# A 1-core kernel of two interleaved passes: all four written orders merged anew, other sample orders, 51 slots kept instead of 42

## The reference

```python
def _gn(v, G=32, eps=1e-5):                       # 32 groups of 24 channels, each over a whole image
    g = v.reshape(B_, H_, W_, G, C_ // G)
    m = jnp.mean(g, axis=(1, 2, 4), keepdims=True)
    s = jnp.var(g, axis=(1, 2, 4), keepdims=True)
    return ((g - m) / jnp.sqrt(s + eps)).reshape(v.shape)

xc = conv2d(xc, conv1_w, conv1_b)                 # 1x1, 768 -> 16 channels
pooled = jnp.mean(xc, axis=(2, 3))
h = pooled @ H_w.T + H_b                          # 4 experts, the two largest kept
g = jax.nn.softmax(jnp.where(mask, h, -jnp.inf), axis=1)
for i in range(E):                                # resize by 2**i, one 3x3 conv, resize back
    ...
gw = jnp.reshape(g, (E, g.shape[0], 1, 1, 1))
out = jnp.sum(Es * gw, axis=0)
out = conv2d(out, conv2_w, conv2_b)               # 1x1, 16 -> 768 channels
x = x + _L0_conv_ref(_gn(x), ...)
```

## Time and profile before

| | |
|---|---|
| median of 3 runs | 1445.71 us (1445.31 to 1447.31) |
| profiled execution, its own time | 1443.26 us |
| its span in the profile | 1441.5 us |
| instructions | 23374 |

### The profile page before, as it was taken

How to read it: one execution, slowest core, us unless ns; L and a number is a source line. 1 busy time by engine, 2 the same in 40 slices (tenths; PEclk the granted TensorE clock), 3 DMA queues, 4 the chain that set the end, 5 groups by cost and what they waited for, 6 DMA issues and landing times.

```text
span 1441.5 us, 23374 instructions
## 1 busy us (share of the span) xinstructions
PE 1108.7 (77%) x8380; PEld 722.4 (50%) x8380; DVE 1028.1 (71%) x2747; ACT 661.8 (46%) x1549; POOL 301.5 (21%) x390
## 2 busy tenths in 40 slices
...
GB/s 342 260 349 316 298 371 315 179 392 345 398 383 414 391 379 352 378 404 404 402 414 409 393 387 284 383 416 416 415 366 390 395 415 415 416 416 416 366 416 386
DMA packets 188159, 539.96 MB, mean 375 GB/s; under 512 B 12810, under 2 KB 12810, under 8 KB 188044
## 3 DMA queue, kind: packets, MB, share of 16 engines
...
...
## 4 chain that ended last, share of the span: by engine, by line
PE 34%; DMA 31%; DVE 18%; ACT 6%; issue 5%; SPq 4%; POOL 1%; ACTq 0%; DVEq 0%; POOLq 0%
DMA x_sb<-in_x 16%; DMA out<-x_sb 15%; PE ring_ps L690 15%; DVE stats L958 9%; PE img_ps L707 8%; DVE x_sb L1042 7%; PE ring_ps L812 5%; SPq L524 3%; ACT xT L834 3%; PE conv_ps L767 2%; SPq L497 1%; PE conv_ps L773 1%; PE ring_ps L799 1%; ACT unread_squares L862 1%; PE ring_ps L721 1%
## 5 line engine op out<-in xcount | busy, mean ns | idle before, releaser
L1042 DVE TENSOR_TENSOR x_sb<-x_sb,ring_ps 128x768 f32<-128x768 f32 x512 | 461.9, 950 | 297.2 <-PE ring_ps L812 169.4
L958 DVE BATCH_NORM_STATS2 stats<-x_sb 128x6 f32<-128x192 f32 x1792 | 473.1, 344 | 43.7 <-DMA x_sb<-in_x 24.7
L812 PE MATMUL ring_ps<-w,es 128*128 128x512 f32 (+1 forms) x1024 | 358.4, 470 | 170.0 <-DVE x_sb L1042 145.3
L834 ACT COPY xT<-ring_ps 128x1024 f32<-128x1024 f32 x384 | 377.2, 1012 | 194.1 <-PE ring_ps L690 132.7
L690 PE MATMUL ring_ps<-ident,x_sb 128*128 128x128 f32 x3072 | 403.5, 285 | 31.6 <-ACT xT L834 11.5
L690 PEld LDWEIGHTS ring_ps<-ident,x_sb 128*128 128x128 f32 x3072 | 352.8, 146 | 108.2 <-issue 59.2
L812 PEld LDWEIGHTS ring_ps<-w,es 128*128 128x128 f32 x1024 | 199.8, 241 | 324.6 <-DVE x_sb L1042 227.6
L707 PE MATMUL img_ps<-xT,w 128*32 128x256 f32 x3072 | 218.3, 393 | 16.6 <-ACT xT L834 14.5
L862 ACT ACTIVATE unread_squares<-x_sb 128x192 bf16<-128x192 f32 x256 | 93.7, 366 | 172.8 <-DVE x_sb L1042 101.7
L898 ACT CAST es<-ring_ps 64x1024 fp32r<-64x1024 f32 x64 | 63.3, 1005 | 201.1 <-PE ring_ps L800 169.6
L624 POOL TENSOR_SCALAR taps<-experts,gates 128x400 f32<-128x400 f32 x16 | 20.5, 1283 | 602.1 <-DVE bias_es L1027 599.9
...
## 6 DMA issues: line engine op xcount, KB each, us to landing
x_sb<-in_x SPq DMA_DIRECT2D x128, 1536.0 KB, 11.3
out<-x_sb ACTq DMA_DIRECT2D x256, 768.0 KB, 10.2
x_sb<-in_x SPq DMA_DIRECT2D x172, 768.0 KB, 9.8
...
wl_raw<-in_L_conv_convl_w SPq DMA_DIRECT2D x8, 9.0 KB
gate_w<-in_L_conv_H_w SPq DMA_DIRECT2D x8, 0.2 KB
...
b_raw<-in_L_conv_conv_b SPq DMA_DIRECT2D x2, 3.0 KB
```

The lines of the kernel that those rows point to most:

```text
L812: last = nc.tensor.matmul(flat_ps[:, buf, part], es4[:, pair_of, QN * n + q], w2[:, part], start=True, stop=True)
L834: nc.scalar.copy(xT[:, at % XT], ring_ps[:, TURN["T", a, n] % RING]).then_inc(xT_copied, 1)
L958: ins = nc.vector.bn_stats(stats[:, c, g, :], group)
L1042: nc.vector.tensor_tensor(x_sb[:, n, 2 * half + q % 2, :], x_sb[:, n, 2 * half + q % 2, :], flat_ps[:, TURN["E", b, t] % RING, 0:D], ALU.a ...
```

## The change

Nothing but text tables changes: the two sample orders, `KEPT`, `TRANSFERS`, `PE_ORDER`, `ACT_ORDER` and `DVE_ORDER`. No instruction of the computation is added or removed, apart from the loads that kept slots save. `KEPT` goes from 42 slots to 51, so that the R transfers go from 172 halves to 154.

```diff
-A_ORDER = [12, 0, 4, 8, 3, 2, 1, 13, 9, 5, 7, 14, 6, 10, 11, 15]
-B_ORDER = [3, 2, 1, 0, 4, 7, 5, 6, 10, 9, 11, 8, 14, 13, 15, 12]
+A_ORDER = [12, 0, 4, 8, 3, 2, 1, 9, 13, 5, 7, 10, 6, 14, 11, 15]
+B_ORDER = [3, 2, 0, 1, 5, 7, 4, 6, 9, 11, 8, 10, 15, 14, 12, 13]
...
-KEPT = {1: 8, 2: 3, 3: 2, 6: 1, 7: 8, 10: 7, 11: 5, 15: 8}
+KEPT = {1: 7, 2: 7, 3: 4, 5: 4, 6: 3, 7: 8, 11: 8, 14: 2, 15: 8}
```

The loads (the old text of the same stretch, then the new):

```diff
-L2.7:1 L1.0:5 L1.1:2 L1.2:3 L1.3:1 L1.4:7 R3.2.0:4.0 R3.2.1:4.1 R3.3.0:0.0 R3.3.1:0.1 L1.5:6 R3.4.0:4.0 R3.4.1:4.1
-L1.6:12 L1.7:10 R3.5.0:0.0 R3.5.1:0.1 R3.6.0:4.0 R3.6.1:4.1 R3.7.0:0.0 R3.7.1:0.1 R2.3.0:0.0 R2.3.1:4.0 R2.4.0:4.1
-R2.4.1:0.1 R2.5.0:9.0 R2.5.1:9.1 R2.6.0:11.0 R2.6.1:8.0 R2.7.0:8.1 L13.0:4 L13.1:0 R2.7.1:11.1 L13.2:9 L13.3:8
-L13.4:11 L13.5:5 L13.6:2 L13.7:3 R0.0.0:1.0 L9.0:7 L9.1:6 L9.2:12 L9.3:10 L9.4:1 L9.5:2 L9.6:3 L9.7:5 L5.0:11 L5.1:8
-L5.2:9 L5.3:0 L5.4:4 L5.5:3 L5.6:5 L5.7:1 L7.0:2 L7.1:10 L7.2:12 L7.3:6 L7.4:7 L7.5:1 L7.6:5 R0.0.1:3.0 R0.1.0:3.1
-R0.1.1:4.0 R0.2.0:4.1 L7.7:0 R0.2.1:3.0 L14.0:9 L14.1:8 R0.3.0:3.1 R0.3.1:4.0 R0.4.0:4.1 R0.4.1:11.0 R0.5.0:11.1
...
+L2.7:1 R3.4.0:5.0 R3.4.1:5.1 R3.5.0:1.0 R3.5.1:1.1 R3.6.0:4.0 R3.6.1:4.1 R3.7.0:0.0 R3.7.1:0.1 L1.0:3 L1.1:2 L1.2:5
+L1.3:1 L1.4:4 L1.5:0 L1.6:9 L1.7:8 R2.7.0:11.0 R2.7.1:11.1 R0.0.0:10.0 R0.0.1:10.1 R0.1.0:12.0 R0.1.1:12.1 R0.2.0:6.0
+R0.2.1:6.1 R0.3.0:7.0 R0.3.1:7.1 R0.4.0:11.0 R0.4.1:11.1 R0.5.0:10.0 R0.5.1:10.1 L9.0:8 R0.6.0:12.0 R0.6.1:12.1 L9.1:6
+R0.7.0:7.0 L9.2:11 R0.7.1:7.1 R1.7.0:10.0 R1.7.1:10.1 L9.3:12 L9.4:7 L9.5:3 L9.6:2 L9.7:5 L13.0:1 L13.1:4 L13.2:0
+L13.3:9 L13.4:2 L13.5:5 L13.6:10 L13.7:3 L5.0:7 L5.1:11 L5.2:12 L5.3:6 L5.4:8 L5.5:3 L5.6:10 L5.7:2 L7.0:5 L7.1:0
+L7.2:9 L7.3:1 L7.4:4 L7.5:2 L7.6:10 L7.7:3 R5.4.0:8.0 R5.4.1:8.1 R5.5.0:7.0 R5.5.1:7.1 R5.6.0:11.0 R5.6.1:11.1
+R5.7.0:12.0 R5.7.1:12.1 L10.0:6 L10.1:8 L10.2:7 L10.3:11 L10.4:12 L10.5:5 L10.6:0 L10.7:9 L6.0:1 L6.1:4 L6.2:2 L6.3:10
+L6.4:3 L6.5:0 L6.6:9 L6.7:5 L14.0:12 L14.1:7 R4.0.0:11.0 R4.0.1:11.1 L14.2:6 L14.3:8 R4.1.0:11.0 R4.1.1:11.1 L14.4:5
+L14.5:9 R4.2.0:11.0 L14.6:0 R4.2.1:3.0 R4.3.0:3.1 R4.3.1:11.1 L14.7:10 R4.4.0:11.0 R4.4.1:3.0 R4.5.0:3.1 R4.5.1:11.1
...
+R6.3.0:1.0 R6.3.1:1.1 R6.4.0:4.0 R6.4.1:4.1 R6.5.0:2.0 R6.5.1:2.1 R6.6.0:1.0 R6.6.1:1.1 R6.7.0:4.0 R6.7.1:4.1
+R9.0.0:2.0 R9.0.1:2.1 R9.1.0:1.0 R9.1.1:1.1 R9.2.0:4.0 R9.2.1:4.1 R9.3.0:2.0 R9.3.1:2.1 R9.4.0:1.0 R9.4.1:1.1
...
```

TensorE's order at the setup, around samples 7, 5, 4 and 6, and around samples 11 and 9 (new text; of the old one only the setup):

```diff
-V Z12 T12.0-5 M12.0-3 T12.6-9 M12.4-7 T12.10 M12.8-9 T12.11-13 M12.10-11 T12.14-15 M12.12-14 T12.16-18 M12.15 T12.19
-M12.16-18 T12.20 M12.19 T12.21-23 M12.20-21 Z0 T0.0 M12.22-23 T0.1-5 M0.0-2 T0.6-7 W M0.3-4 T0.8 M0.5 T0.9 M0.6-9
...
+V T12.0-2 Z12 T12.3-5 M12.0-2 T12.6 M12.3-4 T12.7 M12.5-6 T12.8 M12.7 T12.9-10 M12.8 T12.11 M12.9-10 T12.12 M12.11
+T12.13-14 M12.12 T12.15 M12.13-14 T12.16 M12.15 T12.17-18 M12.16 T12.19 M12.17-18 T12.20 W M12.19 T12.21 M12.20 T12.22
...
+M5.21 T5.23 T7.0 M5.22 T7.1 M5.23 T7.2 G1 Z7 T7.3 H1 M7.0-3 T7.4-6 M7.4 T7.7 M7.5-6 T7.8 M7.7 T7.9 M7.8 T7.10 M7.9
+T7.11 C5.0-6 M7.10-11 T7.12-13 X5.0-1 M7.12-13 E5.0-11 X5.2 E5.12-15 X5.3 E5.16-23 T7.14 E5.24-25 M7.14 T7.15 E5.26-27
...
+X6.2 T14.22-23 M14.22-23 G2 H2 T11.0 E6.12-15 X6.3 E6.16-23 T11.1-2 C9.0-6 E6.24-31 X9.0-1 E9.0-1 Z11 E9.2-3 T11.3
+M11.0-1 E9.4-7 M11.2-3 T11.4 E9.8-9 T11.5 M11.4 T11.6 E9.10-11 M11.5 X9.2 M11.6 T11.7-8 E9.12-13 M11.7 T11.9 M11.8
...
```

VectorE's order at the setup and around the first gates:

```diff
-B12.0.0-27 B12.1.0-27 V B12.2.0-27 B12.3.0-27 F12 B0.0.0-27 B0.1.0-27 B0.2.0-27 B0.3.0-27 F0 B4.0.0-27 W B4.1.0-27
-B4.2.0-27 B4.3.0-27 F4 B8.0.0-27 B8.1.0-27 B8.2.0-27 B8.3.0-27 F8 B3.0.0-27 B3.1.0-27 B3.2.0-27 B3.3.0-27 F3 P0 G0
...
+B12.0.0-13 V B12.0.14-27 B12.1.0-27 B12.2.0-27 B12.3.0-27 F12 B0.0.0-27 B0.1.0-27 B0.2.0-27 B0.3.0-13 W B0.3.14-27 F0
+B4.0.0-27 B4.1.0-27 B4.2.0-27 B4.3.0-27 F4 B8.0.0-27 B8.1.0-27 B8.2.0-27 B8.3.0-27 F8 B3.0.0-27 B3.1.0-27 B3.2.0-27
+B3.3.0-27 F3 P0 B2.0.0-6 G0 B2.0.7-27 B2.1.0-27 B2.2.0-27 B2.3.0-27 F2 L3 A3.0-30 B1.0.0-13 L2 A3.31 B1.0.14-27 A2.0-15
...
```

More of the change, by code:

```diff
@@ L65 @@
[L65 to L74, removed]
@@ L131 @@
-C12.6 E15.20-31 X12.0-1 E12.0-13 X12.2 E12.14-15 X12.3 E12.16-31
+V T12.0-2 Z12 T12.3-5 M12.0-2 T12.6 M12.3-4 T12.7 M12.5-6 T12.8 M12.7 T12.9-10 M12.8 T12.11 M12.9-10 T12.12 M12.11
+T12.13-14 M12.12 T12.15 M12.13-14 T12.16 M12.15 T12.17-18 M12.16 T12.19 M12.17-18 T12.20 W M12.19 T12.21 M12.20 T12.22
+M12.21 T12.23 M12.22 T0.0 M12.23 T0.1-2 Z0 T0.3-5 M0.0-5 T0.6-8 M0.6 T0.9 M0.7-8 T0.10 M0.9 T0.11-12 M0.10 T0.13
+M0.11-12 T0.14 M0.13 T0.15 M0.14 T0.16 M0.15 T0.17-18 M0.16 T0.19-20 M0.17 T0.21 M0.18-19 T0.22 M0.20-21 T0.23 Z4
@@ new lines @@
+T10.12 M10.11 T10.13-14 M10.12 T10.15 M10.13-14 T10.16 M10.15 T10.17-18 M10.16 T10.19 M10.17-18 T10.20 M10.19 T10.21-22
+M10.20 T10.23 M10.21-22 E4.0-2 M10.23 Z6 E4.3 T6.0-3 M6.0-2 T6.4 M6.3 T6.5 E4.4-5 M6.4 T6.6 M6.5 E4.6-7 M6.6 T6.7-8
+M6.7 T6.9-10 M6.8 T6.11 M6.9-10 T6.12 M6.11 T6.13 M6.12 T6.14 E4.8-9 M6.13 T6.15 M6.14 T6.16-17 M6.15 T6.18 E4.10-11
+M6.16-17 X4.2 M6.18 E4.12-13 T6.19 E4.14-15 X4.3 M6.19 T6.20-22 M6.20 T6.23 M6.21-22 T14.0 M6.23 T14.1 E4.16-17 C6.0
+T14.2 E4.18-19 C6.1-2 E4.20-21 C6.3-6 E4.22-23 Z14 T14.3-5 M14.0-2 E4.24-28 M14.3-4 E4.29 M14.5 E4.30-31 T14.6-8 M14.6
@@ new lines @@
+T14.9 M14.7-8 T14.10 M14.9 T14.11 M14.10 X6.0-1 M14.11 T14.12-13 E6.0 T14.14 M14.12-13 E6.1-2 T14.15 M14.14 E6.3 T14.16
+E6.4 M14.15 T14.17 M14.16 E6.5-6 T14.18 M14.17 E6.7 T14.19 M14.18 E6.8 T14.20 M14.19 E6.9-10 T14.21 M14.20 E6.11 M14.21
+X6.2 T14.22-23 M14.22-23 G2 H2 T11.0 E6.12-15 X6.3 E6.16-23 T11.1-2 C9.0-6 E6.24-31 X9.0-1 E9.0-1 Z11 E9.2-3 T11.3
+M11.0-1 E9.4-7 M11.2-3 T11.4 E9.8-9 T11.5 M11.4 T11.6 E9.10-11 M11.5 X9.2 M11.6 T11.7-8 E9.12-13 M11.7 T11.9 M11.8
+T11.10 E9.14-15 M11.9 X9.3 M11.10 T11.11 E9.16-17 T11.12 M11.11 T11.13 E9.18-19 M11.12 T11.14 M11.13 T11.15 E9.20-21
@@ L132 @@
+E12.12-15 X12.3 E12.16-31 X13.0-1 E13.0-11 X13.2 E13.12-15 X13.3 E13.16-31
 """
 ACT_ORDER = """
[L138 to L141 removed]
@@ L177 @@
[L177 to L179 removed]
+S12.0.28-31 S12.1.28-31 S12.2.28-31 S12.3.28-30 T12.0 S12.3.31 T12.1-2 S0.0.28-29 D12 S0.0.30-31 S0.1.28-30 T12.3-6
+S0.1.31 T12.7 S0.2.28 T12.8-10 S0.2.29 T12.11 S0.2.30 T12.12 S0.2.31 T12.13-15 S0.3.28 T12.16-18 S0.3.29 T12.19 S0.3.30
```

202 lines of the change are left out of this document (96 added, 106 removed).

## The result

The changed kernel takes 1459.32 us (median of 4 runs, 1458.62 to 1459.74), the kernel before 1445.51 beside it. The ratio is 1.0099 with a 95% interval of 1.0078 to 1.0121: slower by 1%, where 1432.6 was forecast, and 1.3 us above the range. The profiled execution has a span of 1458.0 against 1441.5, 16.5 us more.

The account below looks back on a forecast made before the run. Transfers, by bytes and by time below their 416 GB/s rate, were taken as the bound: 650 to sample 5's first store + 748.5 + 30 = 1428.4 us span, 1432.6 as measured median; own range 1420 to 1442, full range 1404 to 1458.

Parts of the forecast that it names:

- Traffic: Whole kernel: 51 slots kept instead of 42, 9 fewer reloads, 14.2 MB, 34.0 us less at 416 GB/s.
- Opening: Start to first store: VectorE's new order saves 6 us, bounds 0 and 9.7, first store at 271.4 us.
- W's move: Opening: W falls into VectorE's wait before the fold of sample 0, saving 4 of its 6.7 us.
- Before the first store: Up to the first store: 50 slots moved instead of 53, 11.3 us of transfers lost.
- To T9.0: First store to sample 9's first transpose: 57 slots, 215.5 us, plus 11 lost, bounds 0 and 19; T9.0 at 498.
- The run of pass A: T9.0 to sample 5's first store: 152 us, bounds 142 and 160, 28 slots moved, 46 us without transfers.
- the 8 us to the end of F9: Run of pass A, its first term: F9 ends some 8 us after T9.0.
- the 35.5 for a sample: Run of pass A: three samples at 35.5 us each, 106.5 us together.
- The rest: After sample 5's first store: 198 slots, 748.5 us, transfer-bound, plus 30 us of losses, bounds 10 and 50.
- Slower, 1459: Rival: samples 6 and 9 go through three places with hops of 32 us, adding 26 us; chance 0.22.
- Better overlap: Rival, 1405 us: no loss before T9.0, run of pass A 142, sample 4's hops hidden; chance 0.20.
- The saved bytes come back: Rival, 1445 us: first stretch behind the first store at 382 GB/s, +8, and hops 5 more; chance 0.11.

Follow-up runs that it names:

- Runs 3 and 4: Changed kernel with four kept slots fewer, read again: of sample 5 in the transfer gap, 1457.47 us; of sample 15 where transfers are full, 1476.71 us.
- Run 1: Changed kernel with only ScalarE's opening order edited, sample 0's statistics that need L0.5 put behind later steps of sample 12: 1450.86 us, ratio 1.0037.
- run 2: Changed kernel with W back in its old place in TensorE's and VectorE's order: 1458.70 us, ratio 1.0088.
- run 12: Changed kernel with the old TensorE, ScalarE and VectorE order texts up to the end of pass A over sample 3: 1443.18 us, ratio 0.9982.
- run 11: Run 1 plus two loads of sample 1 before the first store, with two kept slots of sample 3 fewer: 1454.09 us, ratio 1.0056.

## Why the prediction was wrong, step by step

*Traffic: right in its amount.* 154 R transfers, 525.8 MB. In the account by slots of 3.78 us the changed kernel has -34.0 for traffic, +11.3 for the 3 slots fewer moved before the first store, +12.8 for the later first store, and 97.7 us without transfers behind it instead of 71.3, +26.4: together the +16.5 of the two spans. Runs 3 and 4 show why the 34 bought so little: four of the kept slots saved reads at a place where nothing else wanted the transfers.

*Opening, forecast -6: the first step that failed.* It measured +12.8 at the first store. The prediction looked at VectorE's wait before the fold of 0 and at W, and gave W's move 4 us and G0's 2. It followed VectorE's and TensorE's new orders and not ScalarE's. What ScalarE's new order put three steps sooner was a statistic whose load stands behind 21 small ones, and the path of the first store ran through TensorE's stop behind it. Run 1 shows this (10.5 us at the first addition, which is two steps more than undoing the change), run 2 that W is not it, run 12 that the order texts carry all of the loss: with the old ones the first store goes out at 273.8. Another 5.8 us lie between runs 1 and 12. Of these the prediction looked at Z12, with the remark that transposes ahead of it change little; the traces show nothing there and 5.0 us at Z3, at which it did not look. Of the 2 us for G0 1.2 came in: VectorE's wait before the gates is 1.82 us in run 1 and 2.98 in run 12. So the path to the first store had been followed through VectorE alone; +10.5 and +5.8, less the 3.5 us by which run 12 is ahead of the kernel before, make the +12.8.

*Before the first store: right.* 50 slots were moved, and 252 to 288 ran at 95 GB/s where the old slice had 179. The loss was priced as 3 slots; run 11 bears out that the gap could carry two more loads, though not that they would gain time.

*To T9.0: 226.5 forecast, 223.4 measured,* at 407 GB/s on average.

*The run of pass A: right in its mechanism, its size too small, 152 against 171.9,* and beyond the bound of 160. The forecast had 8 us from T9.0 to the end of F9, 106.5 for three samples, 4 for P1 and 34 to the store. Measured, from the end of one fold to the next: 16.5 us to the end of F9, for its last statistics ended only 12 us after T9.0; 40 and 41.5 for samples 13 and 5; 44.5 for sample 7 with its softmax, as the row at 647.46 shows P1 waiting 5.62 us for TensorE's G1, and F7 standing before G1 on VectorE until 656. From there to the store it was 29.5 instead of 34. The steps that failed are two terms: the 8 us to the end of F9 (8.5 short), and the 35.5 for a sample, read from a window full of matmuls (with the softmax 15.5 short over the three); the 34 behind them was 4.5 too much. The forecast let TensorE run as gapless and as fast as in that window. Windows of the changed kernel from fold to fold, samples 13 and 5:

```profile
530.10:570.40 40.30, 38.57 (x393) 26.91 (x391) 33.70 (x134) 35.55 (x99) 0.00 (x0) 0.98 1.03 403
570.40:611.50 41.10, 37.59 (x382) 26.37 (x383) 33.31 (x133) 33.63 (x82) 0.00 (x0) 0.96 0.84 310
```

For 393 matmuls TensorE was busy for 38.57 us, where the earlier trace rows have 35.99, and it stood still besides. VectorE's work of a sample can be added up to the same length, four chunks of statistics of 7.57 us (7.38 and a small one), 5.42 us of wait for TensorE's Z before the fold of sample 5 and 3.75 us of fold, 39.4; but of that the 5.42 are TensorE's, and VectorE was busy for 33.70 us, less than TensorE. Which of the two, or the loads, set these 40 us no run decides; the cause of this size stays open. By the mean of this stretch, 253 GB/s over 171.9 us, 67 us went empty, not 46. The Trainium skill, page "Perfetto Trace Analysis", section Optimization Strategy, says that kernels with several regimes may gain by interleaving them; the 1 GB/s of 648 to 684 shows room for it, but no run here interleaved another sample there, so whether it gains was not measured.

*The rest: 24 us lost where 30 were forecast,* well inside its bounds.

*The rivals.* "Slower, 1459" has the right number for the wrong reason: it was to come from the three places of samples 6 and 9, and these ran at 414 GB/s (972 to 1008). Its sum was off as well: a hop of 32 us is 1.41 times 22.7, not 1.27, which would belong to a hop of 29. "Better overlap" needed a run of 142. "The saved bytes come back" named the first stretch at 382; it ran at 407.
